# One pool of four PSUM banks for scores and side steps, and the chain between two attentions in two overlapping halves

## The reference

```python
# attention 0: 8 heads of 16, causal, with a rank-one term from the first 3 dimensions of q and k
x = layernorm(x + softmax(q @ k.T * 0.25 + head_scale * (q3.dirs)(k3.dirs)) @ v @ w_out)
h = rmsnorm(x, norm1_w)                       # then attention 1: 16 heads of 8, causal
q = rope(h @ Wq.T)
latent = layernorm(h @ Wdkv.T) * ln_g + ln_b  # 64 wide
k, v = rope(latent @ Wuk.T), latent @ Wuv.T
y = x + softmax(q @ k.T / sqrt(8)) @ v @ Wo.T
h = rmsnorm(y, norm2_w)                       # top-1 of 4 experts, hidden width 512
y = y + onehot(argmax(h @ gate.T + gate_b)) . (relu(h @ W1 + b1) @ W2 + b2)
return layernorm(x + y)
```

## Time and profile before

| | |
|---|---|
| median of 3 runs | 676.39 us |
| profiled execution: time, span | 673.76 us, 671.9 us |
| mean granted TensorE clock | 0.954 |
| TensorE matmul busy | 582.0 us (87%) |
| VectorE | 413.1 us (61%) |
| ScalarE | 337.8 us (50%) |
| POOL | 145.5 us (22%) |
| chain that ended last | TensorE 64%, VectorE 20%, DMA 4%, ScalarE 4% |

### The profile page before, as it was taken

One profiled execution on the slowest core, in us unless ns is written; L12 is line 12 of the kernel. 1 busy time (PEld: TensorE's weight loads), 2 busy tenths in 40 slices (PEclk: granted clock), 3 DMA queues, 4 the chain that ended last, 5 costly groups with the idle time before them and its releaser, 6 DMA issues.

```text
span 671.9 us, 10096 instructions
## 1 busy us (share of the span) xinstructions
PE 582.0 (87%) x3668; PEld 279.0 (42%) x3717; DVE 413.1 (61%) x1031; ACT 337.8 (50%) x621; POOL 145.5 (22%) x186
## 2 busy tenths in 40 slices
PE   5578899958777877879999999999989999799994
PEld 3224233424223233424433344455544545357663
DVE  3496987796615968897778878754566402422313
ACT  4234457544463454557766667545546555633330
POOL 7612112313371031135321214011012011101000
PEclk9798899978787998999999999999999999989997
DMA  4856020000044020031313030220000000000000
GB/s 141 210 159 219 26 73 25 2 1 0 32 116 75 1 65 0 3 64 48 85 28 60 6 65 0 31 35 1 2 0 18 2 0 1 17 0 1 17 1 16
DMA packets 27394, 27.69 MB, mean 41 GB/s; under 512 B 6289, under 2 KB 22545, under 8 KB 27090
## 3 DMA queue, kind: packets, MB, share of 16 engines
q1 hardware_dynamic: 26962, 26.26, 16.2%
q0 software_dynamic: 384, 0.79, 0.5%
HBM read 19.40 MB, written 7.34 MB: 40 GB/s over the span
## 4 chain that ended last, share of the span: by engine, by line
PE 64%; DVE 20%; DMA 4%; issue 4%; ACT 4%; POOL 2%; SPq 1%; DVEq 0%; ACTq 0%; POOLq 0%
PE ps L875 13%; PE ps L948 10%; PE ps L858 10%; DVE mparts L1238 10%; PE ps L837 9%; PE ps L1004 8%; PE ps L834 3%; PE ps L937 3%; PE ps L931 2%; ACT pr L1024 2%; DMA qs<-nparts 2%; PE ps L912 2%; PE ps L946 2%; PE ps L886 1%; DVE stats L1147 1%
## 5 line engine op out<-in xcount | busy, mean ns | idle before, releaser
L1024 ACT ACTIVATE pr<-ps 128x512 f32<-128x512 f32 (+1 forms) x456 | 250.3, 576 | 227.9 <-PE ps L858 192.1
L1238 DVE TENSOR_REDUCE mparts<-ps 128x1 f32<-128x512 f32 (+3 forms) x456 | 279.9, 655 | 112.4 <-PE ps L837 111.2
L837 PE MATMUL ps<-ks,qs 125*128 125x512 bf16 (+3 forms) x576 | 170.0, 337 | 12.6 <-DVE mparts L1238 11.1
L858 PE MATMUL ps<-qs,ks 128*128 128x512 bf16 (+3 forms) x532 | 154.6, 332 | 15.7 <-ACT pr L1024 9.2
L752 POOL TENSOR_SCALAR_AFFINE_SELECT pr<-pr 128x512 f32<-128x512 f32 x96 | 61.0, 636 | 369.1 <-ACT pr L1024 368.9
L875 PE MATMUL ps<-pr,vs 128*32 128x512 f32 (+3 forms) x1152 | 126.4, 512 | 0.4 <-POOL pr L752 0.4
L858 PEld LDWEIGHTS ps<-qs,ks 128*128 128x128 bf16 x576 | 50.8, 99 | 143.2 <-ACT pr L1024 92.5
L834 PE MATMUL ps<-cmask,identb 128*128 128x128 bf16 (+2 forms) x259 | 64.9, 251 | 26.9 <-DVE mparts L1238 12.5
L837 PEld LDWEIGHTS ps<-ks,qs 125*128 125x128 bf16 x576 | 55.4, 100 | 53.1 <-DVE mparts L1238 21.2
L948 PE MATMUL ps<-w,work 128*128 128x128 f32 x512 | 74.1, 288 | 0.0
L1089 ACT ACTIVATE work<-ps,b 128x512 f32<-128x512 f32 x64 | 43.8, 686 | 49.1 <-PE ps L1004 48.5
(11 more groups left out here) (119 smaller groups left out, 391.5 us busy)
## 6 DMA issues: line engine op xcount, KB each, us to landing
qs<-scr1q SPq DMA_DIRECT2D x64, 64.0 KB
ks<-scr1k SPq DMA_DIRECT2D x64, 64.0 KB
qs<-scr0q SPq DMA_DIRECT2D x48, 64.0 KB, 2.3
ks<-scr0k SPq DMA_DIRECT2D x36, 64.0 KB, 2.2
scr0q<-parts SPq DMA_DIRECT2D x4, 384.0 KB, 2.8
scr0k<-parts SPq DMA_DIRECT2D x4, 384.0 KB, 3.2
scr1q<-parts SPq DMA_DIRECT2D x4, 384.0 KB, 2.5
scr1k<-parts SPq DMA_DIRECT2D x4, 384.0 KB, 2.6
```

The lines of the kernel that those rows point to most:

```text
L837: last = pe.matmul(bank[:, h, :], queries(F, KMAX, h0 + h, i * P, P), ks[0:KMAX, F % SLOTS, h0 + h, 512 * c:512 * c + w], start=not diagon ...
L858: last = pe.matmul(to[:, h, :], ks[0:KEXP, F % SLOTS, h0 + h, j * P:(j + 1) * P], queries(F, KEXP, h0 + h, qb * 512 + lo, n), start=True, ...
L1024: act.activation(pr[:, st % PSLOTS, h0:h0 + nh, 0:STEPS[st][3]], scores_at(F, v), ACT.Exp, scale=GROUPS[F][0].scale).then_inc(exped, 1)
L1238: dve.tensor_reduce(mparts[:, F % SLOTS, h0:h0 + nh, i, c], maxes_at(F, u), AX_X, ALU.max).then_inc(taken, 1)
```

## The change

The exponentials' scores and the side steps share banks 0 to 3 by least recent use. `between` is made for one half at a time; the halves have windows of their own that overlap. For attention 0's result the two norms are folded: with v the variance, rstd of the layer norm is (v + 1e-5)^-1/2, and the rms norm of the normalised rows gives (v(1 + 1e-6) + 1e-11)^-1/2 on the same centred rows, so that one root over two rows of `rstd` gives both; `hat0` (VectorE) makes the input of attention 1, and `x1` (POOL) the residual. Blocks of attention 1 are now numbered half by half (q and k of half 0, then of half 1), group 4 is loaded in halves, its maxima stand at 0.1 to 0.87, and `zeros` at F - 2 + 0.01. The latent's moments have a tensor of their own.

```diff
@@ -121,8 +123,7 @@
 LAG = 2
 
 
-SCB, SCN = 0, 2
-SIDE = [2, 3]
+SHARED = [0, 1, 2, 3]
 PVB = 4
 MAXB, MAXN = 5, 3
 
...
@@ -132,12 +133,12 @@
 def split_block(M):
 
     n, b = M // 8, M // 4 % 2
-    return (n, b, M // 2 % 2, M % 2) if n else (n, b, M % 2, M // 2 % 2)
+    return n, b, M % 2, M // 2 % 2
 
 
 def block_of(n, b, k, i):
 
-    return 8 * n + 4 * b + (2 * k + i if n else 2 * i + k)
+    return 8 * n + 4 * b + 2 * i + k
 
 
 def backbone():
...
@@ -213,7 +214,7 @@
 
 
 MAX_SPREAD = (-0.2, 0.78)
-MAX_LATE = (0.4, 0.9)
+MAX_LATE = (0.1, 0.87)
 FIRST_MAX = 0.2
 FIRST_SPREAD = (0.25, 0.82)
 FIRST_FILL = 8
...
@@ -271,51 +270,23 @@
-def between(b):
-
-    out = output(0, b, (0, 1))
-    out += both("moments", 0, b) + root("x1", b, (0, 1)) + both("layer_norm", 0, b)
-    out += rms(0, b, (0, 1))
...
+def between(b, i):
+
+    q = block_of(1, b, 0, i)
+    k = block_of(1, b, 1, i)
+    latent = root("latent", b, (i,))
+    return [*output(0, b, (i,)), ("moments", 0, b, i), *root("x1", b, (i,)), ("hat0", b, i), ("x1", b, i),
+            ("feed", "hat0", b, i), ("feat", "hat0", b, i),
+            ("latent", b, i), ("lat_copy", b, i), ("proj", q, 0), ("lat_moments", b, i), ("rotate", q, 0),
+            ("proj", q, 1), *latent[:2], ("rotate", q, 1), *latent[2:], ("rotated", q), ("lat_norm", b, i), ("hi", q),
+            ("lat_turn", b, i), ("r1", q), ("lat_feat", b, i), ("mid", q), ("proj", k, 0), ("lo", q),
+            ("rotate", k, 0), ("store", q), ("proj", k, 1), ("rotate", k, 1), ("rotated", k),
+            ("v_proj", 1, b, i), ("hi", k), ("v_out", 1, b, i), ("r1", k), ("mid", k), ("lo", k), ("store", k)]
...
@@ -353,7 +324,7 @@
 
 def loads(position, F):
 
-    if F >= ATT[0].groups:
+    if F not in HALVED:
         return [(position, ("load", F, k, 2)) for k in range(2)]
     return [(position, ("load", F, k, i)) for i in range(2) for k in range(2)]
 
...
@@ -366,12 +337,15 @@
     out += loads(SECOND[1], 2) + loads(1.02, 3)
     out += [(0.05, ("weights",)), (0.7, ("partners",)), (0.6, ("b2_parts",))]
     out += [(-1.99, ("pads", 0)), (-1.98, ("pads", 1)), (-0.62, ("pads", 2))]
-    out += spread(between(0), *BETWEEN[0]) + loads(BETWEEN[0][1], 4)[1:] + loads(BETWEEN[0][1], 5)
-    out += spread(between(1), *BETWEEN[1])
+    first = loads(0, ATT[0].groups)
+    for i in range(2):
+        out += spread(between(0, i), *BETWEEN[0][i]) + [(NEXT[i], step) for _, step in first[2 * i:2 * i + 2]]
+        out += spread(between(1, i), *BETWEEN[1][i])
+    out += loads(NEXT[2], ATT[0].groups + 1)
     for F in range(6, NF):
         out += loads(F - 2 + 0.02, F)
     out += [(F - 1 + 0.4, ("copy_v", F)) for F in range(1, NF)]
-    out += [(F - 2 + 0.1, ("zeros", F)) for F in range(ATT[0].groups, ATT[0].groups + SLOTS)]
+    out += [(F - 2 + 0.01, ("zeros", F)) for F in range(ATT[0].groups, ATT[0].groups + SLOTS)]
     out += spread(ready(0, (0, 1)) + experts(0, 0) + experts(0, 1), *AFTER)
     out += spread(ready(1, (0,)), *LAST) + [(12.9, ("quiet",))]
     out += spread(experts(1, 0), 13, 14) + spread(ready(1, (1,)), 13, 13.7) + spread(experts(1, 1), 14, 15)
...
@@ -381,7 +355,8 @@
 
 
 SECOND = (-0.5, 0.4)
-BETWEEN = [(2.21, 3.12), (4.21, 5.95)]
+BETWEEN = [[(1.56, 2.7), (2.22, 3.15)], [(3.56, 4.8), (4.22, 5.6)]]
+NEXT = (2.75, 3.17, 3.3)
 AFTER = (8.21, 11.7)
 LAST = (11.71, 12.4)
 SCHEDULE = schedule()
...
@@ -393,29 +368,29 @@
 
     nth, bank_of, freed_by, turn_of = {}, {}, {}, {}
     seen, reader = {}, {}
-    banks, nth_use = [0, 1, *SIDE, PVB], {}
+    banks, nth_use = [*SHARED, PVB], {}
     for s in SCHEDULE:
         kind = s[0]
         seen[kind] = seen.get(kind, 0) + 1
         assert s not in nth
         nth[s] = seen[kind]
-        if kind == "scores" and s[1] == 0 and s[2] < SCN:
-            banks = SIDE
-            freed_by[s] = reader[SCB + s[2]]
-        elif s == ("pv", 0, 0):
+        if s == ("pv", 0, 0):
+            banks = SHARED
             freed_by[s] = reader[PVB]
         elif kind == "quiet":
             banks = list(range(8))
         if kind == "expert" and s[4]:
             bank_of[s] = bank_of[s[:4] + (0,)]
-        elif kind in READER or kind == "proj":
+        elif kind in READER or kind in ("proj", "scores"):
 
             bank = min((b for b in banks if b not in reader or reader[b] in nth), key=lambda b: nth_use.get(b, -1))
             nth_use[bank] = len(nth)
             bank_of[s] = bank
             if bank in reader:
                 freed_by[s] = reader[bank]
-            if kind == "proj":
+            if kind == "scores":
+                reader[bank] = s
+            elif kind == "proj":
                 reader[bank] = ("r1", s[1]) if s[1] < 8 else ("rotate", s[1], s[2])
             else:
                 reader[bank] = (READER[kind],) + s[1:4]
...
@@ -568,7 +544,7 @@
         def scores_at(F, v):
 
             s, _, nh = UNITS[v]
-            bank = ps[:, SCB + (F * NU + v) % SCN, 0:nh * STEPS[s][3]]
+            bank = side("scores", F, v)[:, 0:nh * STEPS[s][3]]
             return bank.rearrange("p (h n) -> p h n", h=nh)
 
         def turn_bank(*step):
...
@@ -784,17 +762,24 @@
                     pool.wait_ge(done["mid"], nth("mid", M))
                     pool.tensor_tensor(parts[:, M % PARTS, 2, :], rest[:, M % 2, :], parts[:, M % PARTS, 1, :],
                                        ALU.subtract).then_inc(done["lo"], 1)
+                elif kind == "x1":
+                    b, i = args
+                    pool.wait_ge(done["root"], nth("root", "x1", b, (i,), 3))
+                    for t in range(TB * b + 4 * i, TB * b + 4 * i + 4):
+                        last = pool.tensor_scalar(x1[:, t, :], xn[:, t, :], mv[:, t, 0:1], rstd[:, 2, t:t + 1],
+                                                  ALU.subtract, ALU.mult)
+                    last.then_inc(done["x1"], 1)
...
@@ -851,8 +836,6 @@
                         pe.wait_ge(rows_in, 48 * (F + 1))
                     else:
                         pe.wait_ge(rows_first, 48)
-                if F or v >= SCN:
-                    pe.wait_ge(exped, nth("scores", F, v) - SCN)
                 to = scores_at(F, v)
                 for h in range(nh):
                     last = pe.matmul(to[:, h, :], ks[0:KEXP, F % SLOTS, h0 + h, j * P:(j + 1) * P],
...
@@ -903,8 +886,11 @@
                     F = GROUPS.index((at, at.gb * (b + 1) - 1))
                     pe.wait_ge(taken, TURN_OF["turn", F, i])
                     tile = [att[:, 4 * i + t, b * C:(b + 1) * C] for t in range(4)]
+                elif src == "hat0":
+                    pe.wait_ge(done["hat0"], nth("hat0", b, i))
+                    tile = [x0[:, TB * b + 4 * i + t, :] for t in range(4)]
                 else:
-                    pe.wait_ge(done["hat"], nth("hat", int(src[3]), b, i))
+                    pe.wait_ge(done["hat"], nth("hat", b, i))
                     tile = [xn[:, TB * b + 4 * i + t, :] for t in range(4)]
                 wait_bank("feed", src, b, i)
                 bank = side("feed", src, b, i)
...
@@ -1155,18 +1138,21 @@
 
 
                 t = slice(TB * b + 4 * blocks[0], TB * b + 4 * blocks[-1] + 4)
-                src, scale, eps, to = ((rstd[:, 3, t], 1.0 / C, 1e-6, 4) if of[:3] == "rms" else
-                                       (mv[:, t, 1], 1.0, 1e-5, 1))
-                v, y, h = rstd[:, 0, t], rstd[:, to, t], rstd[:, 2, t]
+                rows = {"x1": slice(0, 2), "result": slice(0, 1), "latent": slice(1, 2), "rms1": slice(1, 2)}[of]
+                v, y, h = (rstd[:, rows.start + k:rows.stop + k, t] for k in (0, 2, 4))
                 if part == 0:
-                    if of[:3] == "rms":
-                        dve.wait_ge(done["square_sum"], nth("square_sum", int(of[3]), b, blocks[-1]))
+                    if of == "rms1":
+                        dve.wait_ge(done["square_sum"], nth("square_sum", b, blocks[-1]))
+                        link(dve.tensor_scalar(rstd[:, 1, t], rstd[:, 5, t], 1.0 / C, RMS_EPS, ALU.mult, ALU.add))
                     elif of == "latent":
-                        dve.wait_ge(done["lat_moments"], nth("lat_moments", b, 1))
+                        dve.wait_ge(done["lat_moments"], nth("lat_moments", b, blocks[-1]))
+                        link(dve.tensor_scalar(rstd[:, 1, t], lat_mv[:, t, 1], 1.0, LN_EPS, ALU.mult, ALU.add))
                     else:
-                        which = 0 if of == "x1" else 2
-                        dve.wait_ge(done["moments"], nth("moments", which, b, blocks[-1]))
-                    link(dve.tensor_scalar(v, src, scale, eps, ALU.mult, ALU.add))
+                        dve.wait_ge(done["moments"], nth("moments", 0 if of == "x1" else 2, b, blocks[-1]))
+                        if of == "x1":
+
+                            link(dve.tensor_scalar(rstd[:, 1, t], mv[:, t, 1], 1.0 + RMS_EPS, LN_EPS * RMS_EPS, ALU.mult, ALU.add))
```

(55 more changed lines are left out.)

48 lines of the change are left out of this document (26 added, 22 removed).

## The result

The changed kernel takes 695.58 us (694.96 to 695.8, 4 runs) beside 675.6 us before (the median of 4 runs, one more than the three ahead of the forecast): a ratio of 1.0289, with a 95% interval of 1.0258 to 1.0319. The forecast was 646 with a range of 626 to 669. Its profiled execution has a span of 694.1 us and a mean granted clock of 0.961, which is higher than before (0.954): a lower mean clock is not what costs.

What follows compares the result with a forecast made beforehand. Bound by batch 0's squeezed chain between the attentions (35.7 us lost) and TensorE's score-bank waits in plain groups. 673.8 - 21 (batch 0) - 9 (pool) = 643.8 profiled; the median, 2.6 above, gives 646, range 626 to 669.

Steps and rivals of the forecast that it cites:

- Part 1: Scores outside F2 to F5: four shared banks remove 60% of 109 waits of 0.14 us, -9 (0 to -15).
- side readers hold up the scores: Rival, chance 0.08: scores wait for side-step readers of shared banks, 24 of 32 hit, +38 against -30, total 684.
- Part 4: Chain between the attentions: two overlapping halves leave VectorE setting the pace in batch 0's thick part, 3 us lost.
- the 140: Sign of being wrong: F1 to F3 together, 148.3 us before, staying above 140.
- 35.7 us: Time lost on batch 0's chain in F2 and F3 beyond TensorE's own work, to become 14, about -21.
- the clock: Low granted clock after stalls in F2 and F3: up to 15 us lost, 4 left after the change.
- its more numerous root instructions: VectorE roots made per half: 50 instead of 36 instructions, 2.9 us more per batch.
- VectorE takes over: Rival, chance 0.22: roots and maxima still bind; batch 0 regains only 10, the pool 4, total 662.
- Batch 1: Second batch's chain: rms step out, but first half shares VectorE with compressed maxima; 0 (-5 to +4).
- x1 on POOL: Residual made by four POOL scalings per half, 1.0 to 2.5 us per half; cost 0, at worst 10.
- The rows and the keys: Group 4's halved loads: waits for second-half keys lose 3 us, late rows of group 3's maxima lose 2.
- The blocking of VectorE by POOL: Roots beside POOL's x1 and other work: at most 1.3 us per half, 5 in all; 1 taken.

Runs made afterwards that it cites:

- run 4: The kernel before with only the shared pool, each bank chosen by its last reader's place in the written order; 673.2 us, ratio 0.9963.
- run 3: The changed kernel, with a bank chosen by its last reader's place in the written order instead of when last given out; 673.4 us, ratio 0.9958.
- run 12: run 11 with one of three Newton steps left out of the eight x1 and latent roots, an empty step in its place; 667.0 us, ratio 0.9873.
- run 7: run 3 with batch 0's two halves squeezed back into the old window; 671.0 us, ratio 0.9948.
- run 11: run 3 with x1 made late outside the chain, its place kept empty, and batch 0's halves in the old window; 670.7 us, ratio 0.9928.
- run 10: run 3 with x1 made late, its place kept empty, and group 3's maxima spread to 0.92 instead of 0.78 of a group; 674.5 us, ratio 0.9979.
- run 1: The changed kernel with banks apart again, scores on 0 and 1, side steps on 2 and 3; 679.6 us, ratio 1.0048.

## Why the prediction was wrong

**Part 1, the shared pool, had the wrong sign.** I forecast -9 outside F2 to F5 and it is +16 over the kernel, 13 of it in F8 to F11. The step that failed is a wait put at nothing: that of a score for the side reader of its bank. I had read off what two banks cost, a wait of 0.14 us for a slightly late exponential, and had put against it that a bank comes back "after three other uses". That is true of when it was given out and false of when it was read. The experts' banks are held for 8 to 15 steps, so the choice by last use picks just the one whose reader stands one or two steps before. The rival "side readers hold up the scores" had the mechanism and the waits: 24 of 1.6 us, 38 us; there were 26, of 1.4 on the mean, 37.2 us. It had the price wrong, since it took every wait as time lost: the mended order is worth 22.2 us, separate banks 16.0. Its total of 684 was nearest, and still 12 short, because the 30 us of gain that it left to the other parts did not come. I gave it 0.08, though the list of steps from which the distance between a reader and the next user of its bank is counted was there to be read. It was sorted in by plausibility instead of being counted.

**The gain of four banks was over-sized too.** 109 waits x 0.14 x 0.6 = 9 us became, with the order mended, 1.9 on the kernel before (run 4). Of the waits in F6 and F7 42% went, at an estimated 0.08 each; over the kernel the scores' weight load waits for an exponential 87 times in run 3 and 79 in the changed kernel, where 164 were to become fewer than 60. Why a gap that goes gives back only half is not shown; that the next engine in line (ScalarE, VectorE) sets the mean pace would fit. Direction and place were right: F6 30.6, the 0.36 gone. It had been forecast at 29.5 to 30.

**Part 4, the halved chain, gave nothing.** I forecast -21 for batch 0. With banks apart F1 to F3 take 156.0 instead of 148.3; with the mended pool the whole kernel is as long with the halves (673.4) as without (673.2). In the changed kernel F1 to F3 are 150.9, above the 140 that I had named as the sign of being wrong. The step that failed is the budget: 35.7 us had been split by their symptoms (a wait for a square, waits for maxima, the clock, the keys), each was taken out, and the clock was expected to come back by itself. Some did go: ScalarE's 5.19 us wait, half of the keys' (2.53 to 1.24 in the changed kernel), F3 and F5, shorter by 4 and 7 us. But F1+F2 grew: 95.3 before, 102.8 in run 3, with a granted clock in F2 of 0.84 as before, so the clock, which was to give back 11 of its 15 us, gave nothing back there. VectorE is busy 3.2 us more in the two (73.6 against 70.3), near the 2.9 forecast for its more numerous root instructions (50 against 36 per batch); that is less than half of the 7.5. Run 12 shows that the roots' time is on the path (-3.7 for 4.9), runs 7 and 11 that it does not matter where the halves stand. What binds F1+F2 stays open: VectorE's load (against it: its idle time and run 10), or the length of a chain of dependent small steps that holds up the attention in the same written order; no run took these two apart. The rival "VectorE takes over" is not borne out either: its 10 us back for batch 0 did not come.

**Batch 1** (0 forecast, -5 to +4): F4+F5 take 82.9 in run 3 against 88.1, but its first half now lies in F3. Against run 4, with the same rule for the banks, F1+F2 of run 3 are 8.3 longer and F3 to F5 together 12.6 shorter (131.4 against 144.0), in single profiles of kernels with equal medians. Which of it is group 4's earlier maxima and which batch 1's halves is not told apart.

**x1 on POOL** was forecast at 0 and costs 1.2 by the medians, not clear of the noise, though its instructions take 0.82 us and not the 0.25 to 0.6 assumed. **The rows and the keys** cost little: in the changed kernel TensorE waits 2.4 us in all for rows of maxima (2 forecast in F3) and 1.24 for group 4's keys (3 forecast). No run took `zeros` back.

**The blocking of VectorE by POOL** that stood as +1 to +5 is seen again: in run 1 a root's product took 1.26 us from 139.08, while POOL's sum ran 1.26 us from 139.06.

```profile
139.08 1.26 DVE L1163 TENSOR_TENSOR rstd<-rstd 128x4 f32<-128x4 f32 x1
```

```profile
139.06 1.26 POOL L753 TENSOR_TENSOR work<-work 128x512 f32<-128x512 f32 x1 [2.09 <-DVE work L1309]
```

The Trainium skill's rule of an exclusive lock ("SBUF — State Buffer", SBUF: two separate sides) fits the rows, whose ends fall together within 0.02 us. No run took these instructions apart, so what it costs in all stays open.

The best kernel with the same arithmetic is run 11 (670.7 us, 0.7% below before); run 12, one Newton step shorter, is 1.3% below.
